# Cross-attention and FFN block on one core: the second tile's rows loaded earlier, their statistics spread over the gate and up layer, its means spread one chunk earlier, two flags read one step earlier

## The reference, cut to what matters

```python
x = x + xattn(layernorm(x), ctx, ctx, mask)       # softmax(q k^T / 16 + masks) v
n = layernorm(x)
h = silu(n @ w1.T * s1) * (n @ w2.T * s2)         # 256 -> 1024
h = gelu(h @ h1.T * hs1)                          # 1024 -> 1024
h = gelu(h @ h2.T * hs2)                          # 1024 -> 1024
x = x + h @ w3.T * s3                             # 1024 -> 256
```

## Time and profile before

| | before |
|---|---|
| median of 3 runs | 370.94 us (370.41 to 371.08) |
| the profiled execution's own time | 372.69 us |
| its span | 370.7 us |
| PE busy | 361.4 us, 98% |
| DVE busy | 177.9 us, 48% |
| ACT busy | 147.0 us, 40% |
| GpSimd (POOL) busy | 33.9 us, 9% |
| TensorE clock granted | full, 0.997 on average |

### The profile page before, as it was taken

One profiled execution on the slowest core, in us unless ns is written; L12 is line 12 of the kernel. 1 busy time (PEld: TensorE's weight loads), 2 busy tenths in 40 slices (PEclk: granted clock), 3 DMA queues, 4 the chain that ended last, 5 costly groups with the idle time before them and its releaser, 6 DMA issues.

```text
span 370.7 us, 4744 instructions
## 1 busy us (share of the span) xinstructions
PE 361.4 (98%) x1786; PEld 304.6 (82%) x1786; DVE 177.9 (48%) x405; ACT 147.0 (40%) x247; POOL 33.9 (9%) x59
## 2 busy tenths in 40 slices
PE   8899999999999999999999999999999999999994
PEld 7787887878798888888898888888889888888884
DVE  4857425245456652443655752434545652323323
ACT  4799743843135622251143642161122653121210
POOL 7450130000100031000000004000010000000000
PEclk9999999999999999999999999999999999999998
DMA  7899999992710001000331000000001000000001
GB/s 246 324 387 430 355 355 391 387 371 69 242 58 16 3 0 28 2 0 0 110 147 58 1 0 30 0 0 2 0 0 57 2 3 0 0 0 2 0 2 60
DMA packets 12739, 38.34 MB, mean 103 GB/s; under 512 B 2114, under 2 KB 5060, under 8 KB 12356
## 3 DMA queue, kind: packets, MB, share of 16 engines
q1 hardware_dynamic: 11840, 37.12, 27.2%
q10 hardware_dynamic: 868, 0.80, 0.8%
HBM read 35.80 MB, written 13.64 MB: 133 GB/s over the span
## 4 chain that ended last, share of the span: by engine, by line
PE 93%; DVE 3%; ACT 1%; issue 1%; POOL 0%; DVEq 0%; POOLq 0%
PE ring L975 60%; PE ring L949 15%; PE ring L994 8%; PE att L902 2%; PE att L921 2%; PE ring L1107 1%; PE att L892 1%; DVE turned L600 1%; PE att L910 1%; ACT work L476 0%; DVE x_attn L714 0%; DVE h_lo L657 0%; ACT act L517 0%; PE att L1134 0%; DVE h_hi L765 0%
## 5 line engine op out<-in xcount | busy, mean ns | idle before, releaser
L975 PE MATMUL ring<-h_hi,weights 128*128 128x512 f32 x512 | 201.5, 394 | 1.1 <-DVE seg_flags L739 0.9
L975 PE MATMUL ring<-h_lo,weights 128*128 128x512 f32 x512 | 199.4, 390 | 0.0
L975 PEld LDWEIGHTS ring<-h_hi,weights 128*128 128x128 f32 x512 | 96.1, 188 | 21.7 <-issue 1.6
L975 PEld LDWEIGHTS ring<-h_lo,weights 128*128 128x128 f32 x512 | 96.2, 188 | 19.7
L517 ACT ACTIVATE act<-ring,scales 128x512 f32<-128x512 f32 x64 | 44.1, 690 | 160.7 <-PE ring L975 157.2
L765 DVE CAST h_hi<-act 128x512 fp32r<-128x512 f32 x64 | 27.6, 430 | 145.8 <-ACT act L517 137.8
L657 DVE TENSOR_TENSOR h_lo<-act,h_hi 128x512 fp32r<-128x512 f32 x96 | 66.2, 689 | 2.6
L949 PE MATMUL ring<-xn_hi,weights 128*128 128x512 f32 (+1 forms) x140 | 51.6, 375 | 0.2 <-DVE xn_lo L733 0.2
L949 PE MATMUL ring<-xn_lo,weights 128*128 128x512 f32 (+1 forms) x140 | 51.1, 371 | 0.0
L505 ACT ACTIVATE gate<-ring,scales 128x512 f32<-128x512 f32 x32 | 22.0, 689 | 33.7 <-PE ring L949 33.6
L754 DVE SCALAR_TENSOR_TENSOR act<-ring,scales,gate 128x512 f32<-128x512 f32 x32 | 24.0, 749 | 17.4 <-PE ring L949 16.0
(11 more groups left out here) (128 smaller groups left out, 217.5 us busy)
## 6 DMA issues: line engine op xcount, KB each, us to landing
weights_staged<-in_weights SPq DMA_DIRECT2D x22, 512.0 KB, 8.7
weights<-weights_staged SPq DMA_DIRECT2D x22, 512.0 KB, 7.6
x_in<-in_x SPq DMA_DIRECT2D x8, 256.0 KB, 2.9
ctx_cols<-in_ctx_cols SPq DMA_DIRECT2D x8, 256.0 KB, 4.8
ctx_rows<-in_ctx_rows SPq DMA_DIRECT2D x4, 512.0 KB, 7.6
out_dram<-residual SPq DMA_DIRECT2D x16, 128.0 KB, 1.7
turned<-in_x_cols SPq DMA_DIRECT2D x3, 512.0 KB, 8.3
mask<-in_mask SPq DMA_DIRECT2D x3, 256.0 KB
```

What stands on the lines that cost most here:

```text
L975: ins = nc.tensor.matmul(bank[:], w, part[:, k].bitcast(dt), start=(k == 0 and part is h_hi[src]), stop=(k == HC - 1 and part is h_lo[src]))
```

## The change

The loads of tile 1's rows are issued ahead of piece 6's load. DVE takes their statistics one row block at a time, behind chunks 4 to 7 of tile 0's gate and up layer (`next_stats`). In tile 0 the moments move from behind (0, 1) to behind (0, 0), the store of the means on ACT from behind chunk 2 to behind chunk 0, their spread from behind chunk 3 to behind chunk 2, and the centring from behind (0, 6) to behind (0, 5). Flag HID2B is taken before (1, 0), not (1, 1), and flag LAST before (1, 6), not (1, 7). The tests of pieces 14 to 21 move one step earlier each on ACT. Tiles 1 and 2 keep their order, apart from the two flags, which only tile 0 has.

```diff
@@ SyncE
             load_raw(5)
+            sp.wait_ge(x_attn_done, ROWS)
+            load_queries(1)
             order = (*range(RAW, PIECES), *range(RAW))
...
-                if n == FLAG_PIECES[HID1A][1]:
-                    sp.wait_ge(x_attn_done, ROWS)
-                    load_queries(1)
@@ ScalarE, tile
-                        if more and (layer, c) == (0, 2):
+                        if more and (layer, c) == (0, 0 if t == 0 else 2):
                             store_means(t + 1)
-                        if more and (layer, c) == (0, 3):
+                        if more and (layer, c) == (0, 2 if t == 0 else 3):
                             spread_means(t + 1)
...
-            after = ((0, 0), (0, 0), (0, 1), (0, 1), (0, 2), (0, 3), (0, 4), (0, 6), (0, 7), (0, 7), (1, 0), (1, 1),
-                     (1, 2), (1, 3), (1, 4))
+            after = ((0, 0), (0, 0), (0, 1), (0, 1), (0, 2), (0, 3), (0, 4), (0, 5), (0, 6), (0, 6), (0, 7), (1, 0),
+                     (1, 1), (1, 2), (1, 3))
@@ VectorE
+            def next_stats(t, r):
+
+                if r % 2 == 0:
+                    dve.wait_ge(x_loaded[r // 2], 16 * (t + 1))
+                norm_stats(r, x_in)
...
                         dve.wait_ge(hi_done, HC * t + c)
                         lo_part(t, c - 1, 0, c - 1)
+                    if t == 0 and c >= HC - ROWS and c < HC:
+                        next_stats(1, c - HC + ROWS)
...
-                        for flag, before in ((HID1B, (0, 2)), (HID1C, (0, 4)), (HID2A, (0, 7)), (HID2B, (1, 1)),
-                                             (HID2C, (1, 4)), (LAST, (1, 7))):
+                        for flag, before in ((HID1B, (0, 2)), (HID1C, (0, 4)), (HID2A, (0, 7)), (HID2B, (1, 0)),
+                                             (HID2C, (1, 4)), (LAST, (1, 6))):
...
-                        if at == (0, 1):
+                        if at == (0, 0 if t == 0 else 1):
                             wait_stats(t + 1, 0, ROWS - 1)
...
-                        if at == (0, 0):
+                        if t > 0 and at == (0, 0):
                             for r in range(ROWS):
-                                if r % 2 == 0:
-                                    dve.wait_ge(x_loaded[r // 2], 16 * (t + 2))
-                                norm_stats(r, x_in)
-                        if at in ((0, 1), (1, HID2_CHUNKS[2][0])):
+                                next_stats(t + 1, r)
+                        if at in ((0, 0 if t == 0 else 1), (1, HID2_CHUNKS[2][0])):
                             for r in range(ROWS):
                                 norm_moments(r)
-                        if at == (0, 6):
+                        if at == (0, 5 if t == 0 else 6):
                             for b in range(PAIR):
                                 centre(t + 1, b)
```

## The result

The changed kernel takes 369.19 us in the median of 20 runs (367.77 to 370.90); the kernel before, timed beside it, 371.10 (20 runs, 369.82 to 372.92). The ratio is 0.9939 with a 95% interval of 0.9921 to 0.9957: 2.3 us faster (1.6 to 2.9), where 1.4 was forecast. The direction and the three places of the gain were right, the size too small by more than a third of what was measured.

The account below looks back on a forecast made before the run. PE, busy 98% of the span, was taken as the bound, so only its waits and late starts could give time: -0.38 - 1.03 - 0.35 + 0.33 = -1.43 us, 370.94 to 369.5 us, range 369.0 to 370.4.

Parts of the forecast that it names:

- the statistics: Tile 0's gate layer: the second statistic ahead of flag HID1A delays layer 0's start, +0.33 us; the others cost nothing beside it.
- Flag HID2A and the centring (-0.38): Before tile 1's scores: centring one chunk earlier lets DVE write the flag by 62.65, so scores start when due, -0.38 us.
- rival B: Before tile 1's scores: spread means land late, at 63.1, scores start 1.8 us late, total 371.4 us; chance 0.04.
- Flag HID2B (-1.03): Before chunk 2 of layer 1: flag taken before (1, 0) is ready near 71.1, so PE's wait goes, -1.03 us.
- LAST (-0.35): Before the transposes of tile 1's rows: flag taken between chunk 5's and chunk 6's parts, so the delay goes, -0.35 us.
- The bounds: At layer 0's start behind flag HID1A: the statistics' loss lies between 0.10 and 0.40 us.
- The rows' load and the means: Tile 0's transfers: rows loaded ahead of piece 6 and means stored and spread earlier cost nothing; spread expected near 58.5.
- The time outside the span: Profiled execution: its time stands 1.75 us above the runs' median, all outside the span, so the same difference applies to the median.
- A (much given back): Statistics cost 0.40 and flag HID2B's gap is half or fully filled: -0.8 or -0.3 us, 370.1 to 370.6; chance 0.13.
- C (nothing lost at HID1A, 369.3): Layer 0's start loses nothing, -1.76 + 0.1 us for the last low part; inside the forecast, together 0.83.

Follow-up runs that it names:

- the held-up one: The kernel before, unchanged, profiled a second time; PE's gate layer was held up by 0.9 us and the scores started 1.97 us behind the last product.
- the second comparison: The changed kernel, unaltered, timed again against the kernel before: ratio 0.9925 (0.9902 to 0.9948).

## Why the prediction was right or wrong

The forecast was -1.43. One term of its sum, the statistics, failed: it was put at +0.33 and came out at 0.0 in the first pair of profiles, and at 0.1 to 0.2 against executions that nothing else had delayed. One term was missing, the restart behind a stop, 0.25 in all. And one, the centring, was a single draw of something that varies.

*Flag HID2A and the centring (-0.38): right in mechanism, mis-sized.* The scores start when due. Flag HID2A ends at g+45.45, which is where the forecast had it (62.65). But 0.38 was one draw. In five profiles that have the means at the old places and the centring behind chunk 6, the scores were late by 0.38, 1.59, 0.40, 1.74 and 0.45 us, 0.9 on average. In three of them DVE did not wait for the spread, and the 0.4 is the centring standing ahead of the flag; in the other two it waited 1.1 and 1.3 us more. In eight that have both moved up they were never late. I had seen how near it was: the spread landed at 61.9, "just ahead of the centring". What I made of it was a risk for the changed kernel (rival B) and not a cost that the kernel before already paid in some executions. By the mean of these five profiles this is the largest error, about 0.5 us; no timing confirms it.

*Flag HID2B (-1.03) and LAST (-0.35): right.* The starts moved by exactly these amounts, 1.26 to 0.23 and 0.58 to 0.23. What the sum left out is the restart: behind a stop the second product starts 0.31 to 0.33 behind the first instead of 0.23, and the work that followed each of the three stops was longer by 0.10, 0.10 and 0.05. That is another 0.25 us.

*The statistics (+0.33): the step that failed.* The forecast added the second statistic's 0.33 to the start of layer 0 in the profile of before, as if nothing else held that start. Layer 0 does hang on the flag, 1.04 us behind it: that part is shown by the run with two more statistics. But layer 0 started at g+16.95 before and at g+16.96 after. The first profile of before was itself late. ACT waited there for raw piece 4:

```profile
23.42 1.06 ACT L423 ACTIVATE scaled<-turned 128x1024 bf16<-128x1024 uint16 x1 [0.25 <-DMA turned<-in_weights]
```

The rest of ACT's and DVE's work in the gate layer follows it without a gap large enough to win that back. DVE's second gated product stood at g+8.05 and not at g+7.7 to 7.8 as in all others but the held-up one, and the flag ended 0.3 late without any statistic. I added the statistic's 0.33 to a start that another delay had already moved. In the changed kernel that delay was absent and the statistic put the flag at the same place, so the two profiles agree by chance. Against executions without either (g+16.81 and 16.82 in versions of the kernel before, 16.77 and 16.83 in the changed kernel with the flag first) the statistic costs 0.1 to 0.2. What both together would cost isn't shown: no changed kernel was profiled with piece 4 late.

The bounds were 0.10 and 0.40, and I chose near the wrong end. The floor that the Trainium skill gives for a register load ("DMA: Bandwidth & Descriptors", Latency and other measured facts), from which with the branch I had estimated a start at 34.17, 0.71 behind the flag, is less than what was measured: 0.79 us at HID2B, 1.04 at HID1A. It pointed to a small loss, for a reason that the runs don't bear out.

*The rows' load and the means: right.* Neither cost anything that can be seen; the spread landed at 56.3, earlier than the 57.5 to 59.5 that I expected.

*The time outside the span: misread.* The profiled execution's own time was 1.75 above the median, and I put that outside the span. In all timed runs the time stands 1.8 to 2.9 above the span, and in that execution 2.0; the spans of the kernel before have medians of 368.8 to 369.5 in the timed groups, where this one was 370.7. So the 1.75 lay inside the span, and its long end, 4.85 against the usual 2.6, is enough to account for it. The forecast is a difference, so this changed nothing.

*The sum.* Against the first profile, -0.38 - 1.03 - 0.35 - 0.25 + 0.0 = -2.0, the 2.03 of the trace. An estimate for the mean over executions, with -0.9 for the scores and +0.1 for the statistics, is about -2.4, against 2.3 (1.6 to 2.9) measured, and 2.8 (1.9 to 3.6) in the second comparison. The measured times don't choose between -2.0 and -2.4.

*Rivals.* A (much given back) did not come: nothing waited behind flag HID2B. B's mechanism is real, and its price for the scores was about right: in the run with the means back at their old places the spread lands near 62.7, from which B's steps make the scores 1.8 late, and they were 1.7. The change removes it. (B's total, 371.4, left out the +0.33 of the statistics.) C (nothing lost at HID1A, 369.3) came closest in size, partly by luck: layer 0 started no later than in the profile of before only because that one was late itself. A store of 2 KB took 5.5 to 9.6 us in tile 0 in all fourteen profiles, and the same store 2.5 to 3.3 in tile 1 and 1.4 in tile 2, where the weights are in. In the first profile of before it was issued at 46.06, and up to 50.3 no packet of ACT's queue moved, only SP's. The Trainium skill's rule ("DMA: Bandwidth & Descriptors", Queues, rings and completion order), that each DMA engine goes round the queues packet by packet, does not lead one to expect this. Where the 4.2 us are spent, in the DMA engines or before them, the trace doesn't show.

*Open.* Why the transfers of the means land up to 2.5 us apart in the same kernel was not tried; nor whether the mean lateness of the scores over five profiles is that of the timed runs, and that the flags alone time like the whole change is a reason to doubt it. That ACT's wait for piece 4 is what made the first profile's flag late is read from one profile and from its absence in the others, not tried by an edit.

## What to carry to other kernels

Where a step starts right behind a transfer's landing, one profile shows one draw: here the lateness was 0.4 to 1.7 us in five profiles of one order. Profile such a place more than once, and count the removal of that dependence as a gain, not only its creation as a risk. Before a delay is added to a start, ask whether the profile's own start was already held by something else that will not be there next time. A flag that is loaded into a register has to be ready 0.8 to 1.1 us before the product behind its branch is due, by what was measured here, so take it as soon as its sum is made. Count the restart as well as the idle time: each stop of PE here cost 0.05 to 0.1 us beyond it.

## What was not expected of the hardware

The store of the means took 8.2 to 9.6 us in the six profiles that issue it near 46 us, where SP has just issued a burst, and 5.5 to 7.3 in the eight that issue it near 40, before the burst. The spread, 256 KB, took 7.6 to 8.3 us when issued late and 8.5 to 9.6 early. Later in the same profiles, when the weights are in, the store took 2.5 to 3.3 us in tile 1 and 1.4 in tile 2, and the spread 3.0 to 3.4. This row is from tile 2 in the first profile of before:

```profile
means<-mean_scaled ACTq DMA_DIRECT2D x1, 2.0 KB, 1.4
```

Much of the difference passes before the transfer begins. In the first profile of before, ACT's queue moved its first packet 4.2 us after the issue, in that of the change 3.6 us after it (issued at 39.93), and in tile 1 of the kernel before under 1 us after it. So 2 KB in one queue pay for the traffic of another, though the trace doesn't show where they wait.

The delay from a flag's end to PE's first product was 0.79 to 0.80 us at HID2B in the five profiles in which chunk 2 waited for it, and 1.03 to 1.09 at HID1A in the eight profiles in which layer 0 waited for it. Why the two places differ wasn't tried.
